# FP4 feed-forward: the rounding constant, the normalisation and the residual leave VectorE, and its rounding is split over two tiles

## The reference

```python
def fp4_quant_dequant(x):
    xb = x.reshape(shape[:-1] + (shape[-1] // BLOCK, BLOCK))     # BLOCK = 16
    scale = jnp.max(jnp.abs(xb), axis=-1, keepdims=True) / 6.0
    scale = jnp.maximum(scale, jnp.float32(1e-12))
    xn = xb / scale
    idx = jnp.searchsorted(_MID, jnp.abs(xn))
    q = _GRID[idx] * jnp.sign(xn) * scale                        # _GRID = 0, 0.5, 1, 1.5, 2, 3, 4, 6
    return q.reshape(shape)

def fp4_linear(x, w):
    return jnp.einsum('bsk,nk->bsn', fp4_quant_dequant(x), fp4_quant_dequant(w))

# x = x + _L1_ffn_ref(_layernorm(x), ...), where _L1_ffn_ref(x) is
gate = fp4_linear(x, w_gate)          # 256 -> 704
y = fp4_linear(x, w_up)               # 256 -> 704
h = jax.nn.silu(gate) * y
return fp4_linear(h, w_down)          # 704 -> 256
```

## Time and profile before

| what | value |
|---|---|
| median of 3 runs | 3720.13 us (3717.05 to 3722.45) |
| the profiled execution, its time | 3720.78 us |
| the profiled execution, its span | 3719.0 us |
| share of the span busy | PE 88%, PEld 66%, DVE 69%, ACT 37%, POOL 26% |
| mean granted clock of TensorE | 0.940 |
| first transfer of the last stage issued | 3320.65 us from the span's start |
| last y of the last stage begins on VectorE | 3716.36 us |

### The profile page before, as it was taken

The page is one execution under the profiler, slowest core; times in us unless marked ns, Lnnn a source line. Parts: engine busy times, 40 slices in busy tenths (PEclk is TensorE's granted clock), DMA queues, the critical chain, the costliest instruction groups (busy, mean ns, idle before and its releaser), DMA issues. The chain is left out here.

```text
span 3719.0 us, 141826 instructions
## 1 busy us (share of the span) xinstructions
PE 3255.9 (88%) x62854; PEld 2466.6 (66%) x62854; DVE 2569.9 (69%) x5676; ACT 1383.9 (37%) x3203; POOL 951.1 (26%) x1051
## 2 busy tenths in 40 slices
PE   7775999997799999998999999989999999848888
PEld 4564999996566666766676676666666766535555
DVE  6873111111788788878887887778878888828887
ACT  2221222222345444444444444445444444421111
POOL 2343222221222322232222223222322232211110
PEclk9886999998899999999999999999999999979998
DMA  2116666673000000000000000000000000010000
GB/s 68 53 49 223 182 187 188 185 250 90 8 8 7 12 8 8 10 10 8 7 10 9 8 7 10 9 8 7 11 9 8 8 12 6 5 46 16 23 23 13
DMA packets 98174, 168.17 MB, mean 45 GB/s; under 512 B 15400, under 2 KB 71976, under 8 KB 97312
## 3 DMA queue, kind: packets, MB, share of 16 engines
q1 hardware_dynamic: 76976, 136.07, 11.0%
q0 software_dynamic: 19440, 21.97, 4.2%
q10 hardware_dynamic: 1152, 1.06, 0.1%
HBM read 118.86 MB, written 38.09 MB: 42 GB/s over the span
## 5 line engine op out<-in xcount | busy, mean ns | idle before, releaser
L1066 POOL TENSOR_TENSOR da_M<-da_M,da_decay 128x512 f32<-128x512 f32 x256 | 269.4, 1075 | 732.5 <-DVE da_prev_end L1178 408.6
L1373 ACT COPY da_Ub<-da_U 32x256 f32<-32x256 f32 x1024 | 412.1, 402 | 17.1
L1203 DVE TENSOR_TENSOR da_eGn<-da_eGn,da_z 128x30 f32<-128x30 f32 (+14 forms) x960 | 352.1, 367 | 32.9
L1202 DVE TENSOR_TENSOR da_z<-da_eGn 128x30 f32<-128x30 f32 (+14 forms) x960 | 344.2, 359 | 27.6
L1668 PE MATMUL da_C<-da_Ub,da_Km 128*64 128x256 f32 x2048 | 298.9, 411 | 3.8 <-issue 1.6
L840 PEld LDWEIGHTS le_ps_qkv<-le_scr,le_up 128*128 128x128 f32 x2272 | 265.9, 193 | 4.8 <-ACT le_scr L670 1.8
L840 PE MATMUL le_ps_qkv<-le_scr,le_up 128*128 128x128 f32 x2272 | 267.9, 277 | 1.2 <-ACT le_scr L670 1.2
L1499 PE MATMUL da_unit<-early_buffer,da_xnT 128*128 128x512 f32 x512 | 259.2, 630 | 5.5 <-ACT da_xnT L1319 2.3
L1506 PE MATMUL da_unit<-da_xnT,early_buffer 128*128 128x128 f32 x2048 | 247.1, 277 | 9.9 <-ACT da_eGn L1358 9.9
L1506 PEld LDWEIGHTS da_unit<-da_xnT,early_buffer 128*128 128x128 f32 x2048 | 238.2, 192 | 19.0 <-ACT da_eGn L1358 17.4
L1226 DVE TENSOR_TENSOR da_M<-da_C,da_M 128x512 f32<-128x512 f32 x256 | 176.2, 688 | 72.5 <-PE da_C L1668 68.6
(11 more groups left out here) (299 smaller groups left out, 7057.1 us busy)
## 6 DMA issues: line engine op xcount, KB each, us to landing
le_up<-in_upT SPq DMA_DIRECT2D x71, 1024.0 KB, 5.1
le_scr<-moe_slots SPq DMA_DIRECT2D x71, 129.0 KB, 4.3
le_down<-in_downT SPq DMA_DIRECT2D x8, 1024.0 KB, 12.1
early_buffer<-in_x SPq DMA_DIRECT2D x16, 256.0 KB, 4.0
moe_acc<-le_y SPq DMA_DIRECT2D x32, 128.0 KB, 2.3
da_x<-moe_acc SPq DMA_DIRECT2D x128, 32.0 KB, 1.8
stream<-da_xz SPq DMA_DIRECT2D x128, 32.0 KB, 1.6
stream<-da_y POOLq DMA_DIRECT2D x128, 32.0 KB, 3.0
```

The source lines that it names most:

```text
L1066: ins = nc.gpsimd.tensor_tensor(st_, st_, decay[:, par, rec, 2 * g:2 * g + 2].rearrange("p a b -> p (a b)").unsqueeze(2).to_broadcast([P, ...
L1202: c.link(tt(t, Xm[:, s + 1:C, s:s + 1].to_broadcast([P, below, s]), Xm[:, s:s + 1, 0:s].to_broadcast([P, below, s]), ALU.mult))
L1203: c.link(tt(Xm[:, s + 1:C, 0:s], Xm[:, s + 1:C, 0:s], t, ALU.add))
L1373: ins = nc.scalar.copy(Ub[rows_of(b), :, :, b, :], U[rows_of(b), rec])
```

## The change

ScalarE takes over four things. It normalises the four tiles of a trip (`normalised`, with a factor and a bias per row, for which GpSimd makes two more small products). It makes the rounding constant from the exponent, as what lies above the smallest one (`steps_above`, a Relu). It copies y out of PSUM (`result`). The residual x comes into the down product's PSUM bank as a product of the identity with x. VectorE's rounding of a tile falls into `exponents(n)`, up to the mask, and `levels(n)`, which are run one tile apart; TensorE's `transpose_h` and `down` follow `gate_up` at a distance of two tiles in place of one.

```diff
@@ gpsimd
-                nc.gpsimd.tensor_tensor(rstd[:], ve[:], mhalf[:].to_broadcast([P, UN]), ALU.pow).then_inc(rstd_ready, 1)
+                if t > 0:
+                    pool.wait_ge(z_ready, t * UN)
+                pc.link(nc.gpsimd.tensor_tensor(rstd[:], ve[:], mhalf[:].to_broadcast([P, UN]), ALU.pow))
+                pc.link(nc.gpsimd.tensor_tensor(nb[:], mv[:, :, 0], rstd[:], ALU.mult))
+                nc.gpsimd.tensor_tensor(nb[:], nb[:], neg[:], ALU.mult).then_inc(nb_ready, 1)
...
@@ vector
             def round_z(t):
-                dve.wait_ge(rstd_ready, t + 1)
-                for u in range(UN):
-                    ins = nc.vector.tensor_scalar(z[:, u, :], x[:, t % XB, u, :], mv[:, u, 0:1], rstd[:, u:u + 1], ALU.subtract, ALU.mult)
-                c.link(ins)
+                dve.wait_ge(z_ready, (t + 1) * UN)
...
+            def exponents(n):
+                k = n % 2
+                src = in_blocks(h[:, k, :])
+                c.link(nc.vector.tensor_reduce(amax[:, 0:NB], src, AX, ALU.max, apply_absolute_value=True))
+                c.link(nc.vector.tensor_scalar(hscl[:, k], amax[:, 0:NB], 1.0 / FP4_MAX, 1e-12, ALU.mult, ALU.max))
+                c.link(nc.vector.reciprocal(inv[:, 0:NB], hscl[:, k]))
+                c.link(nc.vector.scalar_tensor_tensor(in_blocks(ratio[:, k]), src, TIES_DOWN, per_block(inv[:, 0:NB]), ALU.mult, ALU.mult))
+                if n >= 2:
+                    dve.wait_ge(above_ready, n - 1)
+                nc.vector.tensor_scalar(expo[:, k].bitcast(U32), ratio[:, k].bitcast(U32), EXPONENT, None, ALU.bitwise_and).then_inc(expo_ready, 1)
+
+            def levels(n):
+                k = n % 2
+                dve.wait_ge(above_ready, n + 1)
+                if n >= 1:
+                    dve.wait_ge(qh_ready, n)
+                c.link(nc.vector.scalar_tensor_tensor(level[:], above[:, k], HALF_STEP, ratio[:, k], ALU.add, ALU.add))
+                c.link(nc.vector.scalar_tensor_tensor(level[:], level[:], HALF_STEP, above[:, k], ALU.subtract, ALU.subtract))
                 if n >= 2:
                     dve.wait_ge(hT_psum, n - 1)
...
+                nc.vector.tensor_tensor(in_blocks(qh[:, k, :]), in_blocks(level[:]), per_block(hscl[:, k]), ALU.mult).then_inc(qh_ready, 1)
...
-                if n >= 2:
-                    result(n - 2)
                 hidden(n)
+                exponents(n)
                 if u == 0 and t + 1 < TRIPS:
                     norm(t + 1)
-                round_h(n)
+                if n >= 1:
+                    levels(n - 1)
                 if u == 1 and t + 1 < TRIPS:
                     round_z(t + 1)
...
@@ scalar
+            def normalised(t):
+                act.wait_ge(nb_ready, t + 1)
+                if t > 0:
+                    act.wait_ge(z_scaled, t)
+                for u in range(UN):
+                    nc.scalar.activation(z[:, u, :], x[:, t % XB, u, :], ACT.Identity, bias=nb[:, u:u + 1], scale=rstd[:, u:u + 1]).then_inc(z_ready, 1)
+
+            def steps_above(n):
+                act.wait_ge(expo_ready, n + 1)
+                if n >= 2:
+                    act.wait_ge(qh_ready, n - 1)
+                nc.scalar.activation(above[:, n % 2], expo[:, n % 2], ACT.Relu, bias=below[:], scale=HALF_STEP).then_inc(above_ready, 1)
+
+            def result(n):
+                t, u = divmod(n, UN)
+                act.wait_ge(y_psum, n + 1)
+                if t > 0:
+                    act.wait_ge(stored[u], 16 * t)
+                nc.scalar.copy(y[:, u, :], ps_y[:, 0:D]).then_inc(y_ready, 1)
...
                 silus(n)
-                if n >= 1:
-                    copy_hT(n - 1)
+                if n >= 2:
+                    copy_hT(n - 2)
+                steps_above(n)
                 if u == 3 and t + 1 < TRIPS:
                     for p in range(2):
                         copy_zT(t + 1, p)
...
+                if n >= 2:
+                    result(n - 2)
+                if u == 0 and t + 1 < TRIPS:
+                    normalised(t + 1)
...
@@ tensor
+                nc.tensor.matmul(ps_y[:, 0:D], ident[:], x[:, (n // UN) % XB, n % UN, :], start=True, stop=False)
                 for k in range(IC):
                     width = min(P, I - k * P)
-                    ins = nc.tensor.matmul(ps_y[:, 0:D], hqT[0:width, n % 2, k, :], downT[0:width, k, :], start=(k == 0), stop=(k == IC - 1))
+                    ins = nc.tensor.matmul(ps_y[:, 0:D], hqT[0:width, n % 2, k, :], downT[0:width, k, :], start=False, stop=(k == IC - 1))
```

More of the change, by code:

```diff
@@ L1855, in fp4_feed_forward @@
         h = m.sb("h", [P, 2, I]); qh = m.sb("qh", [P, 2, I]); silu = m.sb("silu", [P, 2, I])
-        ratio = m.sb("ratio", [P, WIDE]); expo = m.sb("expo", [P, WIDE]); magic = m.sb("magic", [P, WIDE]); level = m.sb("level", [P, WIDE])
-        amax = m.sb("amax", [P, WIDE // FP4_BLOCK]); scl = m.sb("scl", [P, WIDE // FP4_BLOCK]); inv = m.sb("inv", [P, WIDE // FP4_BLOCK])
+        ratio = m.sb("ratio", [P, 2, I]); expo = m.sb("expo", [P, 2, I]); above = m.sb("above", [P, 2, I]); level = m.sb("level", [P, I])
+        hscl = m.sb("hscl", [P, 2, I // FP4_BLOCK]); zexpo = m.sb("zexpo", [P, WIDE]); below = m.sb("below", [P, 1]); neg = m.sb("neg", [P, UN]); nb = m.sb("nb", [P, UN])
+        amax = m.sb("amax", [P, WIDE // FP4_BLOCK]); inv = m.sb("inv", [P, WIDE // FP4_BLOCK])
         zratio = m.sb("zratio", [P, WIDE]); zmagic = m.sb("zmagic", [P, WIDE]); zlevel = m.sb("zlevel", [P, WIDE]); zscl = m.sb("zscl", [P, WIDE // FP4_BLOCK])
@@ L1893, in _ @@
             blocks = lambda a: a.rearrange("p (b e) -> p b e", e=FP4_BLOCK)
+            nc.gpsimd.memset(below[:], -HALF_STEP).then_inc(made, 1)
+            pc.link(nc.gpsimd.memset(neg[:], -1.0))
             pool.wait_ge(loaded, 32)
@@ L1931, in norm @@
                 dve.wait_ge(x_loaded[b], 16 * (t // XB + 1))
+                if t > 0:
+                    dve.wait_ge(nb_ready, t)
                 for u in range(UN):
@@ L2024, in _ @@
                         copy_zT(t + 1, p)
-            copy_hT(NT - 1)
+                if n >= 2:
+                    result(n - 2)
+                if u == 0 and t + 1 < TRIPS:
+                    normalised(t + 1)
+            for n in (NT - 2, NT - 1):
+                copy_hT(n)
+                result(n)
         @block.tensor
@@ L2075, in _ @@
                 gate_up(n)
-                if n >= 1:
-                    transpose_h(n - 1)
+                if n >= 2:
+                    transpose_h(n - 2)
                 if u == 3 and t + 1 < TRIPS:
                     transpose_z(t + 1)
-                if n >= 1:
-                    down(n - 1)
-            transpose_h(NT - 1)
-            down(NT - 1)
+                if n >= 2:
+                    down(n - 2)
+            for n in (NT - 2, NT - 1):
+                transpose_h(n)
+                down(n)
 _OUT = (4, 1024, 256)
```

26 lines of the change are left out of this document (11 added, 15 removed).

## The result

The changed kernel takes 3749.05 us (median; 3736.84 to 3752.56), the kernel before 3719.56 us (3717.05 to 3722.45) beside it: a ratio of 1.0073, 95% interval 1.0049 to 1.0098. It is slower by 29.5 us. The forecast was 3767 us, its range 3729 to 3785.

The account below looks back on a forecast made before the run. VectorE's queue was taken to set the trip. Seven trips (+41.6 us), start (+1.2) and end (+3.9) sum to 46.7 on 3720.8 us: 3767 us, range 3729 to 3785, its own range 3752 to 3784.

Parts of the forecast that it names:

- the y wait: Kernel before, once a trip: TensorE's down product of the second tile waits 3.83 us for VectorE's y, behind `round_z`.
- the first rival: GpSimd-VectorE port collision costs nothing: 3752 us, chance 0.24; with the clock also staying at 2.4 GHz, 3730 us, 0.07.
- Steps 1 and 2: Trip's start: statistics done at 11.07 us, TensorE's tile 10.18; normalisation ends at 14.75, before the second Silu: no delay.
- Step 3: Next trip's normalisation: GpSimd's small operations collide with VectorE's last steps, making `hidden(4t+1)` 2.1 us later, at 18.4.
- Step 4: From `hidden(4t+1)` VectorE has no pause for 20.92 us, until tile 4t+1 is rounded at 39.3.
- The 7.74 us beside GpSimd: VectorE, end of `round_z` to end of `expo` while GpSimd rounds z: stays 7.74 us, for 4.37 elsewhere.
- Step 5: Trip's end, `hidden(4t+3)` through constant, z copy and down product: 9.54 us, plus 3.1 of clock loss; trip 52.0.
- the long case: TensorE's longer slow stretch at low clock behind a wait: 4.6 us lost, against 1.66; mean taken 3.1.
- Start: Last stage, from root to first block maximum: 2.5 us now, 3.7 after, +1.2.
- End: Last trip: tiles 30 and 31 follow at 5.35 us each, y at 53.4 against 49.5: +3.9.
- The third rival: VectorE's 5 us reach the end, decided by the copy of z: trip 43.0, 3705 us, chance 0.08.
- The fourth rival: No difference: no collision, full clock, constant of 0.63, overlapping z copy: 45.5 a trip, 3722 us, chance 0.04.

Follow-up runs that it names:

- the fourth experiment: Changed kernel with nine unused identity products between z's two halves, keeping TensorE busy in the wait: 3742.38 us, ratio 1.0047.
- the repeat: The changed kernel measured once more, unaltered: 3753.17 us, ratio 1.0091 to the kernel before.
- the first experiment: Changed kernel with ScalarE's copies of z put ahead of the rounding constant: 3733.07 us, ratio 1.0021.
- the tenth: On the eighth experiment: levels of tile 4t+1 ahead of exponents of tile 4t+2, that tile's constant one tile later: 3707.81 us, ratio 0.9971.
- the twelfth experiment: Edits of the ninth and the tenth together on the eighth experiment, whose orders the last trip keeps: 3694.11 us, ratio 0.993.
- the eighth experiment: On the first experiment: identity product ahead of the wait for the tile's copies, levels of tile 30 first in the last tile: 3732.86 us, ratio 1.0026.
- ninth: On the eighth experiment: first half of z turned and copied ahead of tile 4t+1: 3707.78 us, ratio 0.9968.

## Why the prediction was right, point by point

The direction held, and of the mechanism this much: the wait at z's second half, forecast at about 4.1 us, is 4.12; the copies stand behind the constant; the y wait is gone; VectorE's busy time in the stage falls by 39.4 us for "about 40". The sizes held less well: the stage lost 30.7 us where 46.7 were forecast, and the time lies under the forecast's own range (3752 to 3784), in the part of the whole range that belongs to the first rival. Along the walk:

- Steps 1 and 2: the root starts 11.15 us into the trip (forecast 11.07); TensorE's tile is 10.06 (10.18).
- Step 3: right in kind, too large. From the root's start to the normalisation 2.70 in place of 1.60: +1.1, not +2.1. Root and second product were held (1.60 and 0.72), the first product was not (0.20): the one row of another stage that I took for each of the three does not hold for all. `hidden(4t+1)` is done at 17.3 us, not 18.4. The rule of the Trainium skill ("SBUF — State Buffer", "Who interferes with whom"), by which the two engines would take turns, gave the upper bound, 2.5 us; the trace agrees with it in part only, 1.1 us.
- Step 4: from the end of `hidden(4t+1)` (3545.30 + 0.95) to the turning at 3567.14 are 20.9 us (20.92). The 7.74 us beside GpSimd stay: from the end of `round_z` (3555.95 + 0.69) to that of `expo` (3562.29 + 2.14) are 7.79.
- Step 5: 3.78 us from z's second half to the next gate at the full clock (3577.35 to 3581.13 in the fourth experiment; 4.11 taken). The clock's loss is 1.9 a trip by the fourth experiment, not 3.1: I had given the long case half the trips, and neither profile of the changed kernel has one.

The trip: 52.0 - 1.1 - 0.3 - 1.2 = 49.4, measured 49.49, just under the 50 to 53 that were named as the sign. The forecast's 41.6 us of trips are 22.7 (six of 3.44, and 2.1 in the first).

- Start: +1.7 in place of +1.2, +0.8 in the repeat; this stretch varies from 23.9 to 27.4 us over all the profiles and is not settled further.
- End: +6.3 in place of +3.9. The walk was right up to tile 30 (turned from 42.0 us into the last trip on, forecast 42.3); then I counted 5.35 us for each of two tiles, and the first takes 8.07, since the clock falls there too. Those 2.7 us are the miss. The fourth experiment shows them: with the clock up there, the last stretch is 55.27 us.

The two errors have opposite signs, so that part of the one is hidden by the other, which is luck; the time came out 18 us under the forecast. It lies near the 3752 us of the first rival, but not for its reason: that rival had no collision and 3.1 us of clock, and the runs have 1.1 us of collision and 1.9 of clock. The third rival's point (the copy of z decides) is what the first experiment shows: with the copy in time the loss inside the trips is gone, but a trip is then only 0.3 us shorter than before, and the 43.0 us that this rival forecast came only with further moves (43.15 in the tenth). The fourth rival is out. Of the rivals' sums two come out otherwise than written: the third gives 3704 us, and the fourth, as it is described, about 45.9 us a trip; neither touches the outcome.

What I had not asked is which of the four moves does the harm. The residual alone costs 18.7 us and moves the wait from y to the turning; the constant in front of the copies costs 21; measured on different kernels, the two don't add up. Neither is a matter of the work itself: the twelfth experiment has all four moves and is 0.7% faster than before.

## What to carry to other kernels

Work taken off the bounding engine pays only if the longest chain gets shorter; measure that chain from one mark of the trip to another (38.2 to 38.4 us in the changed kernel and the first, eighth and ninth experiments) in every variant, since whatever is saved beside it comes back as a wait. When an operation goes to another engine's queue, look at what is queued behind it and who waits for that: here one Relu of 0.88 us, put two lines later, was worth 21 us. And where TensorE stands before a long product, price the clock as well as the wait.

## What was not expected of the hardware

- The stages ahead, with the same code in all the kernels, let the last one begin between 3305.97 and 3336.01 us in the fourteen profiles, and the time of one kernel scatters by 10 us and more, while the last stage of the changed kernel is 429.03 and 429.01 us in its two profiles. Why they move was not tried.
- A wait of the same length does not always lower the clock. Behind the late Silus TensorE waits 2.00 us; the down product then took 2.95 us in all the trips of the fourth experiment and 4.58 to 4.63 in three of the first. There the loss cost nothing: it fell into the wait for VectorE's chain (0.57 us left of 2.2), and these were the shortest trips, 44.6 us.
- GpSimd's operations on 128 x 4 numbers beside VectorE's three last steps are not held alike: 1.60, 0.20 and 0.72 us in one trip, 1.60, 0.95 and 0.20 in one of the eighth experiment. VectorE's steps beside them took 0.89, 0.89 and 0.93 us in the first of these trips, where 0.89 is what they take with GpSimd idle.
